# Quantised cross-attention of a six-stage decoder on one core: maxima on VectorE, scores read from PSUM by ScalarE

## The chip, the cores and the metric

One NeuronCore of a Trainium2 chip runs the whole program. The metric is the device time of one execution in microseconds (us); the median of several executions is given.

## What is computed

Two decoder layers, each with self-attention, cross-attention and a feed-forward part, every part followed by a residual add and a layer norm: six stages on x of 2 x 256 tokens and 256 columns. The change is in stage 5, the quantised cross-attention:

```python
q = _fq_sym(q * scale, axis=-1)       # round(q / s) * s, s = max|q| / 127 per token and head
k = _fq_sym(k, axis=-1)
v = _fq_sym(v, axis=2)
attn = softmax(einsum('bhqd,bhkd->bhqk', q, k))
attn = _fq_unsigned(attn, axis=-1)    # round(attn / s) * s, s = max / 255 per row
out = einsum('bhqk,bhkd->bhqd', attn, v) @ Wp + bp
```

All 512 queries look at all 1024 context tokens, with 16 heads of 16 columns. Since a row's largest probability becomes 255, exp(score - max + ln 255) written as a whole number is the quantised probability; the sum of the exponentials isn't needed for the scale of a step, only to divide the result.

## The kernel before, in words

The program is written engine by engine, with semaphores by hand; each engine works through its list in order. Stages 1 to 4 end at about 233 us, stage 5 runs from there to about 346 us, stage 6 (64 experts) fills the rest.

Stage 5 is cut into 64 **units**: a block i of 128 queries (4 of them) and one head h (16). A unit's way:

- TensorE, `scores(u)` (line 1098): two matmuls of 128x512 into two banks of PSUM, units in turn in banks 0-1 and 2-3. The scores are products of whole numbers (the queries' rounded values); the query scale `qsc` is still to be multiplied. They wait for the maximum of unit u-2, which has emptied the two banks. TensorE issues them three units ahead of its loop.
- VectorE, `maximum(u)` (line 1629): one custom instruction that multiplies by `qsc`, stores the scores in SBUF (`sx`, three buffers in turn) and gives the row's maximum; an instruction that reads its accumulator follows. It waits for the scores, and for the exponential of unit u-3, which frees `sx`.
- GpSimd (line 563): the bias, ln 255 minus the maximum.
- ScalarE (line 724): the exponential of `sx` with that bias, written as int16 into `px` (PX = 4 buffers in turn), with the row's sum, read from the accumulator by a second instruction. It waits for the bias, and for the turn of unit u-4 out of the same `px` buffer.
- The turn (128 queries x 1024 keys become 8 blocks of keys x queries), in one of two ways. By DMA: SyncE issues one DMA transpose (line 407) from `px` to `pTx` (PT = 6 buffers in turn) and waits for `px` and for the products that free `pTx`. Or "by scalar", for every ninth unit from unit 4 and the last two: TensorE transposes into banks 4 and 5 (line 1108) and ScalarE copies to `pTx` (`evac_px`, line 747).
- TensorE, `apply(m)` (line 1123): for two units at once, 16 matmuls with the quantised values, into bank 6 or 7.

Per block come the division by the sums (`turn_z`, `spread_z`, `normalise`), the projection, the residual add and the norm (`add`, `norm_stats`, `norm_scale`), between units of the next block. The blocks' quantised queries are themselves turned by DMA (`turn_queries`, line 393): blocks 0 and 1 in stage 4, blocks 2 and 3 in stage 5, before the transposes of unit 8 and unit 11 in SyncE's list. Block 3's queries need stage 4's last norm, so TensorE projects them in its step 10 (`queries`, line 798), behind the scores of unit 13; VectorE adds a bias (line 1523) and quantises them behind the maximum of unit 12.

Of the kernel before, what the change touches and what calls it, by code (L numbers as in the profile page):

```python
# [58 lines left out]
PT = 6  # L59
SHARE = ((4,), 9)  # L60
GROUP = 4
# [7 lines left out]
def build(nc, t, out):  # L69

    with ExitStack() as ctx:
# [160 lines left out]

        sx = carve("a", 2 * N, [3, B * M])
        pTx = [carve(where, at + k * KT * P // 2, [KT * P], I16)
# [38 lines left out]
        def by_scalar(u):  # L273

            return u % SHARE[1] in SHARE[0] or u >= TT * HX - 2

        def query_bank(i):

            return bank(6)[:, D:2 * D] if i == 1 else bank(7)[:, 0:D]

        def unit5(u):
# [146 lines left out]
        def _(pool):  # L428
# [116 lines left out]
            for n in range(1, STAGES + 1):  # L545
# [13 lines left out]
                if n == 5:  # L559

                    for u in range(TT * HX):
                        pool.wait_ge(sem("maxx_ready"), u + 1)
                        pool.tensor_scalar(nbx[:, u:u + 1], mxx[:, u:u + 1], -1.0, math.log(255.0),  # L563
                                           ALU.mult, ALU.add).then_inc(sem("biasx_ready"), 1)
# [29 lines left out]
        def _(act):  # L594
# [120 lines left out]
            def stage5():  # L715

                act.wait_ge(sem("o1_ps"), len(items1) // 2)
                for u in range(TT * HX):
                    i, h = unit5(u)
                    act.wait_ge(sem("biasx_ready"), u + 1)  # L720
                    if u >= PX:

                        px_free(act, u - PX)
                    act.activation(px[:, u % PX, :], sx[:, u % 3, :], ACT.Exp, bias=nbx[:, u:u + 1],  # L724
                                   accum_out=zx[:, i, h:h + 1]).then_inc(sem("px_ready"), 1)
# [68 lines left out]
        def _(pe):  # L794
# [291 lines left out]
            def stage5():  # L1086
# [3 lines left out]
                def scores(u):  # L1090
                    i, h = unit5(u)
                    if u >= 2:

                        pe.wait_ge(sem("maxx_ready"), u - 1)
                    if h == HEADS[0]:
                        pe.wait_ge(sem("queries_turned"), 32 * (i + 1))
                    for half in range(2):
                        mm = pe.matmul(bank(2 * (u % 2) + half), qTx[i][:, h * P:(h + 1) * P].bitcast(BF16),  # L1098
                                       kTx[:, h // 2, half * 512:(half + 1) * 512], start=True, stop=True)
                    mm.then_inc(sem("sx_ps"), 1)  # L1100
# [50 lines left out]
                for u in range(units + 3):  # L1151
# [32 lines left out]
                    if u == units + 2:  # L1184
# [4 lines left out]
                        mm.then_inc(sem("zfx_ps"), 1)  # L1189
                        pe.wait_ge(sem("maxx_ready"), units)  # L1190
                        for i in range(TT - 1):
# [3 lines left out]
                    if u == units - 2:  # L1195

                        pe.wait_ge(sem("maxx_ready"), units - 1)
                        for i in range(TT - 1):
                            pe.wait_ge(sem("x_ready"), nth(5, i))
                            for c in range(DC):  # L1200
                                mm = pe.transpose(bank(i // 2)[:, D * (i % 2) + c * P:D * (i % 2) + (c + 1) * P],
                                                  x_tok[1][:, i, c * P:(c + 1) * P], ident[:])
# [79 lines left out]
        def _(dve):  # L1282
# [338 lines left out]
            def stage5():  # L1621
                def maximum(u):

                    dve.wait_ge(sem("sx_ps"), u + 1)
                    i, h = unit5(u)
                    if u >= 3:

                        dve.wait_ge(sem("px_ready"), u - 2)
                    dve.tensor_tensor_reduce(sx[:, u % 3, :], bank(2 * (u % 2), 2), zero[:].broadcast_to([P, B * M]),  # L1629
                                             qsc[:, i, h:h + 1], LOWEST, ALU.add, ALU.max,  # L1630
                                             mxx[:, u:u + 1]).then_inc(sem("maxx_ready"), 1)

# [47 lines left out]
                for i in range(TT - 1):  # L1680
                    dve.wait_ge(sem("xT_ps"), nth(5, max(i, 1)))
                    slot = bank(i // 2)[:, D * (i % 2):D * (i % 2) + D].rearrange("p (c t) -> p c t", c=DC)
                    dve.tensor_copy(xT[1][:, :, i * P:(i + 1) * P], slot).then_inc(sem("xT_ready"), 1)
# [112 lines left out]
```

## Time and profile before

| | us |
|---|---|
| median of 3 runs | 448.67 (448.04 to 448.78) |
| the profiled execution, its own time | 446.82 |
| its span, first to last instruction | 445.0 |

| engine | busy us | share of the span |
|---|---|---|
| TensorE, matmuls | 369.6 | 83% |
| TensorE, weight loads | 219.1 | 49% |
| VectorE | 304.7 | 68% |
| ScalarE | 211.5 | 48% |
| GpSimd | 110.5 | 25% |

The shares are means over six stages with different limits: in stage 6 TensorE is full (9 tenths in each of the last slices) while VectorE is at 2 to 3 tenths; in stage 5 TensorE stands at 7 to 8 tenths, VectorE and ScalarE at 8 to 9 and the DMA engines at 7 to 9. The chain of waits that ended last goes through TensorE for 55% of the span, VectorE 14%, DMA 10%, ScalarE 6%. In the rows below, PE is TensorE, DVE VectorE, ACT ScalarE, POOL GpSimd, SPq the queue of SyncE; a group's row reads: line, engine, operation, out<-in with shapes, xcount | busy us, mean ns of one | idle us of the engine just before them, and what ended it.

### The profile page before, as it was taken

Reading aid. Unit: us, or ns where it says so; the run is one execution under the profiler, and the core shown is the slowest. Engines: PE = TensorE matmul, PEld = TensorE weight load, DVE = VectorE, ACT = ScalarE, POOL = GpSimd, SP = SyncE. Lnnn points to the kernel's source line nnn. Section 1 sums busy time; section 2 is a strip of 40 time slices with the busy share of each in tenths; the row PEclk is TensorE's granted clock in tenths of the full one; section 3 lists DMA queues with packets and bytes.
Section 4 is the critical chain, followed back from the end, with each engine's and each line's share of the span. In section 5 each row is a group of like instructions: output and inputs, shape, how many; then the busy total and the mean of one; then the engine's idle time right before and its main releaser. Section 6 shows DMA issues by size and latency. Waiting matters only on the chain.

```text
span 445.0 us, 6798 instructions
## 1 busy us (share of the span) xinstructions
PE 369.6 (83%) x2355; PEld 219.1 (49%) x2379; DVE 304.7 (68%) x636; ACT 211.5 (48%) x540; POOL 110.5 (25%) x214
## 2 busy tenths in 40 slices
PE   5978859599987999989976657778669897999993
PEld 2535547444443566657753323335337444556662
DVE  3896988989624587889779888998993652222335
ACT  2781412462245665765526758988985420111100
POOL 8237778648471000000111101211120000000002
PEclk9998996889999599999989886896998999999997
DMA  8994111850000000020026789997998004122111
GB/s 255 292 371 91 1 3 2 330 236 1 0 1 0 1 2 1 1 49 0 4 47 104 143 156 157 159 159 144 161 174 233 3 5 149 40 55 47 49 47 47
DMA packets 81857, 41.42 MB, mean 93 GB/s; under 512 B 70496, under 2 KB 77600, under 8 KB 81376
## 3 DMA queue, kind: packets, MB, share of 16 engines
q1 hardware_dynamic: 79520, 40.93, 38.2%
q0 software_dynamic: 2304, 0.07, 1.5%
q8 instruction: 19, 0.31, 0.3%
q14 instruction: 14, 0.11, 0.1%
HBM read 21.58 MB, written 2.88 MB: 55 GB/s over the span
## 4 chain that ended last, share of the span: by engine, by line
PE 55%; DVE 14%; DMA 10%; issue 9%; POOL 6%; ACT 6%; SPq 0%; POOLq 0%; DVEq 0%; ACTq 0%
PE ps L798 28%; PE ps L1254 6%; DMA area_b<-area_a 6%; PE ps L1037 5%; PE ps L1048 4%; POOL deltas L508 4%; DVE area_a L1629 3%; ACT area_a L724 3%; PE ps L970 2%; PE ps L1031 2%; PE ps L1098 2%; ACT area_a L699 2%; DMA area_b<-deltas 2%; DMA deltas<-entry_w,small 1%; DVE stats L1374 1%
## 5 line engine op out<-in xcount | busy, mean ns | idle before, releaser
L1629 DVE CUSTOM_DVE_ANT_0 area_a<-ps,zero,small 128x1024 f32<-128x1024 f32 x64 | 79.5, 1274 | 7.8 <-PE ps L1098 3.8
L724 ACT ACTIVATE area_a<-area_a,small 128x1024 int16<-128x1024 f32 x64 | 73.1, 1143 | 22.6 <-POOL small L563 13.7
L699 ACT ACTIVATE area_a<-ps,small 128x256 f32<-128x256 f32 (+1 forms) x128 | 52.0, 430 | 31.8 <-DVE small L1571 28.0
L798 PE MATMUL ps<-xT_odd,early 128*128 128x512 f32 (+2 forms) x136 | 58.3, 571 | 0.9 <-DVE area_b L1711 0.8
L486 POOL TENSOR_SCALAR var_eps<-meanvar 128x1 f32<-128x1 f32 x24 | 7.0, 293 | 198.5 <-DVE meanvar L1375 198.3
L1711 DVE TENSOR_TENSOR area_b<-ps,area_b 128x512 f32<-128x512 f32 x16 | 11.0, 690 | 50.5 <-ACT area_b L773 50.5
L1571 DVE TENSOR_REDUCE small<-ps 128x4 f32<-128x1024 f32 (+1 forms) x24 | 29.3, 1222 | 20.2 <-PE ps L1037 17.3
L773 ACT ACTIVATE area_b<-ps 128x512 f32<-128x512 f32 x16 | 9.5, 596 | 61.9 <-PE ps L798 61.9
L798 PEld LDWEIGHTS ps<-xT_odd,early 128*128 128x128 f32 x136 | 24.9, 190 | 26.3 <-issue 22.3
L798 PE MATMUL ps<-area_b,xT_even 128*128 128x512 f32 x64 | 31.4, 637 | 5.2 <-ACT area_b L676 5.2
L563 POOL TENSOR_SCALAR small<-small 128x1 f32<-128x1 f32 x64 | 12.7, 198 | 84.5 <-DVE small L1629 84.4
L1580 DVE COPY area_b<-ps 128x512 f32<-128x512 f32 x48 | 30.9, 680 | 1.7 <-PE ps L1048 1.5
L1254 PE MATMUL ps<-area_a,area_b 128*128 128x256 f32 x128 | 29.8, 380 | 2.6 <-DVE area_b L1740 2.6
L1098 PE MATMUL ps<-area_b,area_a 128*128 128x512 bf16 x58 | 18.6, 398 | 15.4 <-DVE small L1629 14.6
L1123 PE MATMUL ps<-area_b 128*32 128x128 f16 x512 | 23.0, 240 | 8.3 <-DMA area_b<-area_a 7.4
L1254 PEld LDWEIGHTS ps<-area_a,area_b 128*128 128x128 f32 x128 | 24.2, 190 | 11.3 <-issue 7.8
L508 POOL DMA_INDIRECT deltas<-entry_w,small x16 | 26.2, 1636 | 13.9 <-DVE small L1334 8.0
L1048 PE MATMUL ps<-ident,area_a 128*128 128x128 f32 x192 | 29.1, 298 | 0.5 <-DVE area_b L1580 0.4
L1037 PE MATMUL ps<-area_a,area_b 32*128 32x256 f32 (+1 forms) x160 | 29.2, 475 | 0.0
L1048 PEld LDWEIGHTS ps<-ident,area_a 128*128 128x128 f32 x192 | 22.7, 151 | 12.8 <-issue 6.6
L1123 PEld LDWEIGHTS ps<-area_b 128*32 128x32 f16 x512 | 17.0, 106 | 22.3 <-issue 20.4
L699 ACT ACTIVATION_READ_ACCUMULATOR area_a<-ps,small 128x1 f32 x128 | 27.4, 214 | 0.0
(278 smaller groups left out, 637.9 us busy)
## 6 DMA issues: line engine op xcount, KB each, us to landing
early<-in_w_up_dram SPq DMA_DIRECT2D x1, 4096.0 KB, 13.5
area_b<-gates_out SPq DMA_DIRECT2D x16, 256.0 KB, 3.1
deltas<-area_b SPq DMA_DIRECT2D x1, 2112.0 KB, 17.7
area_b<-deltas SPq DMA_DIRECT2D x2, 1024.0 KB, 5.8
area_a<-in_w_down_dram SPq DMA_DIRECT2D x1, 2048.0 KB, 11.5
early<-in_ctxT_dram SPq DMA_DIRECT2D x1, 1024.0 KB, 13.1
early<-in_ctx_dram SPq DMA_DIRECT2D x1, 1024.0 KB
area_b<-area_a SPq DMA_TRANSPOSE x59, 3.3
```

The source lines that it names most:

```text
L508: pool.indirect_dma_start(out=deltas, out_offset=bass.IndirectOffsetOnAxis(ap=place[:, j:j + 1], axis=0), in_=entry_w[:, j, :], in_offset= ...
L699: a = act.activation(p1[:, n % 2, x * nk * P:(x + 1) * nk * P], scores1(n)[:, x * nk * P:(x + 1) * nk * P], ACT.Exp, bias=nmx1[:, n % 2, x ...
L724: act.activation(px[:, u % PX, :], sx[:, u % 3, :], ACT.Exp, bias=nbx[:, u:u + 1], accum_out=zx[:, i, h:h + 1]).then_inc(sem("px_ready"), 1)
L798: mm = pe.matmul(dst, lhsT(c), rhs(c), start=start and c == 0, stop=stop and c == DC - 1, **kw)
L1037: mm = pe.matmul(dst, qT1[rows, c, i * P:(i + 1) * P], kT1[rows, c, heads, kt * P:(kt + 1) * P], start=False, stop=b == nk - 1)
L1048: mm = pe.transpose(bank(4 + x)[:, y * P:(y + 1) * P], p1[:, n % 2, (4 * x + y) * P:(4 * x + y + 1) * P], ident[:])
L1098: mm = pe.matmul(bank(2 * (u % 2) + half), qTx[i][:, h * P:(h + 1) * P].bitcast(BF16), kTx[:, h // 2, half * 512:(half + 1) * 512], start= ...
L1123: mm = pe.matmul(dst, ivh[:, k * HX + h, :], p[:, k * P:(k + 1) * P], start=first and k == 0, stop=not first and k == KT - 1)
L1254: mm = pe.matmul(proj(i), hidden[:, g % 2, i * P:(i + 1) * P], w_down[:, g, :], start=g == 0 and i % 2 == 0, stop=g == NG - 1, skip_group_ ...
L1571: dve.tensor_reduce(nmx1[:, n % 2, 0:8 // nk], scores1(n).rearrange("p (h k) -> p h k", k=nk * P), AX.X, ALU.max, negate=True).then_inc(se ...
L1580: dve.tensor_copy(pT1[:, n % 4, 4 * x * P:4 * (x + 1) * P], bank(4 + x)).then_inc(sem("pT1_ready"), 1)
L1629: dve.tensor_tensor_reduce(sx[:, u % 3, :], bank(2 * (u % 2), 2), zero[:].broadcast_to([P, B * M]), qsc[:, i, h:h + 1], LOWEST, ALU.add, A ...
```

## The change

1. VectorE takes only the maximum, straight from PSUM, with its sign turned (`tensor_reduce`); `sx` is gone.
2. ScalarE reads the scores from PSUM, with `qsc` as the scale of the exponential beside the bias. GpSimd's bias multiplies the (negated) maximum by `qsc`.
3. The scores of a unit lie in three places in turn, banks 0-1, 2-3 and 4-5. `scores(u)` waits for the exponential of unit u-3 instead of the maximum of unit u-2.
4. Only units 62 and 63 are turned by TensorE and ScalarE. Units 4, 13, 22, 31, 40, 49 and 58 are now turned by DMA as well.
5. At the end of the stage the first three blocks' transposes go to banks 2 and 3, and wait for an exponential instead of a maximum.

```diff
-SHARE = ((4,), 9)
...
-            return u % SHARE[1] in SHARE[0] or u >= TT * HX - 2
+            return u >= TT * HX - 2
...
+        def scores5(u):
+
+            return bank(2 * (u % 3), 2)
...
-                        pool.tensor_scalar(nbx[:, u:u + 1], mxx[:, u:u + 1], -1.0, math.log(255.0),
+                        i, h = unit5(u)
+                        pool.tensor_scalar(nbx[:, u:u + 1], mxx[:, u:u + 1], qsc[:, i, h:h + 1], math.log(255.0),
...
-                    act.activation(px[:, u % PX, :], sx[:, u % 3, :], ACT.Exp, bias=nbx[:, u:u + 1],
+                    act.activation(px[:, u % PX, :], scores5(u), ACT.Exp, bias=nbx[:, u:u + 1], scale=qsc[:, i, h:h + 1],
...
-                    if u >= 2:
-
-                        pe.wait_ge(sem("maxx_ready"), u - 1)
+                    if u >= 3:
+
+                        pe.wait_ge(sem("px_ready"), u - 2)
...
-                        mm = pe.matmul(bank(2 * (u % 2) + half), qTx[i][:, h * P:(h + 1) * P].bitcast(BF16),
+                        mm = pe.matmul(scores5(u)[:, half * 512:(half + 1) * 512], qTx[i][:, h * P:(h + 1) * P].bitcast(BF16),
...
-                        pe.wait_ge(sem("maxx_ready"), units)
+                        pe.wait_ge(sem("xT_ready"), nth(5, TT - 2))
...
-                        pe.wait_ge(sem("maxx_ready"), units - 1)
+                        pe.wait_ge(sem("px_ready"), units - 2)
...
-                    i, h = unit5(u)
-                    if u >= 3:
-
-                        dve.wait_ge(sem("px_ready"), u - 2)
-                    dve.tensor_tensor_reduce(sx[:, u % 3, :], bank(2 * (u % 2), 2), zero[:].broadcast_to([P, B * M]),
-                                             qsc[:, i, h:h + 1], LOWEST, ALU.add, ALU.max,
-                                             mxx[:, u:u + 1]).then_inc(sem("maxx_ready"), 1)
+                    dve.tensor_reduce(mxx[:, u:u + 1], scores5(u), AX.X, ALU.max, negate=True).then_inc(sem("maxx_ready"), 1)
```

What moves in the engines' lists shows on TensorE around the first block change (line 1098, in the new kernel 1101, are the scores; 1123, now 1126, the products with the values; 1108 the turn of a probability unit; 1131 and 1137, now 1134 and 1140, the turn and spread of the sums). Before:

```order
L1123 MATMUL ps<-area_b 32x128 [waits turned_3,turned_2,qx_ready]
L1123 MATMUL ps<-area_b 32x128 x15
L1098 MATMUL ps<-area_b 128x512 [waits maxx_ready]
L1098 MATMUL ps<-area_b 128x512
L1131 MATMUL ps<-ident,small 16x128 [waits sumsx_out,rzx_ready]
L1098 MATMUL ps<-area_b 128x512 [waits maxx_ready]
L1098 MATMUL ps<-area_b 128x512
L1123 MATMUL ps<-area_b 32x128 [waits turned_1,turned_0]
L1123 MATMUL ps<-area_b 32x128 x15
L1098 MATMUL ps<-area_b 128x512 [waits maxx_ready]
L1098 MATMUL ps<-area_b 128x512
L1108 MATMUL ps<-ident_b,area_a 128x128 [waits pTx_act,px_ready]
```

And now:

```order
L1126 MATMUL ps<-area_b 32x128 [waits turned_1,turned_0,qx_ready]
L1126 MATMUL ps<-area_b 32x128 x15
L1101 MATMUL ps<-area_b 128x512 [waits px_ready]
L1101 MATMUL ps<-area_b 128x512
L1134 MATMUL ps<-ident,small 16x128 [waits sumsx_out,rzx_ready]
L1101 MATMUL ps<-area_b 128x512 [waits px_ready]
L1101 MATMUL ps<-area_b 128x512
L1126 MATMUL ps<-area_b 32x128 [waits turned_3,turned_2]
L1126 MATMUL ps<-area_b 32x128 x15
L1101 MATMUL ps<-area_b 128x512 [waits px_ready]
L1101 MATMUL ps<-area_b 128x512
L1140 MATMUL ps<-rzTx,pair_rows 128x128 [waits rzTx_ready]
```

The order is the same but for the turn, which is gone; each unit's scores wait for ScalarE (`px_ready`) instead of VectorE (`maxx_ready`).

SyncE's list from unit 0 on (line 407, now 409, a unit's probabilities; 393, now 395, the queries of blocks 2 and 3). Before:

```order
L407 DMA_TRANSPOSE area_b<-area_a 128x8x128 [waits px_ready] x5
L407 DMA_TRANSPOSE area_b<-area_a 128x8x128 [waits ox_ps,px_ready] x2
L393 DMA_TRANSPOSE area_b<-area_a 128x8x128 [waits qstack_ready]
L393 DMA_TRANSPOSE area_b<-area_a 128x8x128
L407 DMA_TRANSPOSE area_b<-area_a 128x8x128 [waits ox_ps,px_ready] x3
L393 DMA_TRANSPOSE area_a<-area_a 128x8x128 [waits qstack_ready]
L393 DMA_TRANSPOSE area_a<-area_a 128x8x128
L407 DMA_TRANSPOSE area_b<-area_a 128x8x128 [waits ox_ps,px_ready] x45
```

And now:

```order
L409 DMA_TRANSPOSE area_b<-area_a 128x8x128 [waits px_ready] x6
L409 DMA_TRANSPOSE area_b<-area_a 128x8x128 [waits ox_ps,px_ready] x2
L395 DMA_TRANSPOSE area_b<-area_a 128x8x128 [waits qstack_ready]
L395 DMA_TRANSPOSE area_b<-area_a 128x8x128
L409 DMA_TRANSPOSE area_b<-area_a 128x8x128 [waits ox_ps,px_ready] x3
L395 DMA_TRANSPOSE area_a<-area_a 128x8x128 [waits qstack_ready]
L395 DMA_TRANSPOSE area_a<-area_a 128x8x128
L409 DMA_TRANSPOSE area_b<-area_a 128x8x128 [waits ox_ps,px_ready] x51
```

One transpose more stands ahead of the queries of block 2, and 51 instead of 45 behind those of block 3.

## Rows read from the trace of the kernel before

**Rows 1.** The page, part 5: groups of the quantised stage and their idle time.
```profile
L1629 DVE CUSTOM_DVE_ANT_0 area_a<-ps,zero,small 128x1024 f32<-128x1024 f32 x64 | 79.5, 1274 | 7.8 <-PE ps L1098 3.8
L724 ACT ACTIVATE area_a<-area_a,small 128x1024 int16<-128x1024 f32 x64 | 73.1, 1143 | 22.6 <-POOL small L563 13.7
```

**Rows 2.** Windows of the quantised stage: busy by engine, clock, DMA share, GB/s.
```profile
core 0: us, PE busy (x) PEld busy (x) DVE busy (x) ACT busy (x) POOL busy (x), PEclk, DMA share, GB/s
233.00:261.00 28.00, 17.05 (x156) 8.43 (x159) 25.84 (x56) 18.01 (x30) 4.46 (x18) 0.91 0.70 123
261.00:336.00 75.00, 55.91 (x576) 28.62 (x583) 65.61 (x116) 65.76 (x116) 12.09 (x56) 0.86 0.92 159
```

**Rows 3.** Line 407, the DMA transposes of probabilities: issue duration, who waited, landing.
```profile
L407 SPq DMA_TRANSPOSE area_b<-area_a x55: 1231/1283/2644, 235.8 to 334.9; - x55
...
  ACT area_a L724: 8.5, 11
...
DMA to landing us min/median/max: 3.0/3.3/4.8
```

**Rows 4.** Timeline of SyncE's queue: start, us from first start to last end, count.
```profile
258.37 2.62 SPq L393 DMA_TRANSPOSE area_a<-area_a  x2
...
261.09 75.01 SPq L407 DMA_TRANSPOSE area_b<-area_a  x45
```

**Rows 5.** The same queue in five stretches between transposes that TensorE made.
```profile
267.83 9.56 SPq L407 DMA_TRANSPOSE area_b<-area_a  x6
...
281.69 8.69 SPq L407 DMA_TRANSPOSE area_b<-area_a  x6
...
294.43 8.89 SPq L407 DMA_TRANSPOSE area_b<-area_a  x6
...
308.89 8.12 SPq L407 DMA_TRANSPOSE area_b<-area_a  x6
...
317.73 12.28 SPq L407 DMA_TRANSPOSE area_b<-area_a  x8
```

**Rows 6.** DMA queues: all of 308.9 to 317 us; instruction loads of 261 to 336 us.
```profile
q1 hardware_dynamic: 5289, 1.32, 86.1%
...
q8 instruction: 5, 0.08, 0.5%
```

**Rows 7.** Groups by form: VectorE maxima; ScalarE from SBUF or PSUM, with scalars.
```profile
L1571 DVE TENSOR_REDUCE small<-ps 128x4 f32<-128x1024 f32 x16 | 19.6, 1222 | 11.6 <-PE ps L1037 11.5
...
L688 ACT ACTIVATE area_a<-ps,head_sel 128x512 f32<-128x512 f32 x8 | 4.8, 688 | 4.9 <-PE ps L798 4.9
...
L653 ACT ACTIVATE area_a<-area_a,small 128x512 f32<-128x512 f32 x4 | 2.9, 717 | 2.3 <-issue 2.3
...
L636 ACT ACTIVATE area_a<-ps,bvx 128x512 f32<-128x512 f32 x4 | 2.7, 673 | 1.0 <-PE ps L798 1.0
...
L661 ACT ACTIVATE area_a<-ps 128x512 f32<-128x512 f32 x4 | 2.4, 597 | 3.5 <-PE ps L907 3.1 <-issue 0.4
```

**Rows 8.** Timeline at the last block's queries and the unit after them.
```profile
252.45 0.93 PE L1098 MATMUL ps<-area_b,area_a 128*128 128x512 bf16 x2 [0.60 <-DVE small L1629]
...
255.19 0.42 DVE L1523 TENSOR_TENSOR area_b<-ps,bqx 128x256 f32<-128x256 f32 x1 [1.60 <-PE ps L798]
...
258.26 1.28 DVE L1629 CUSTOM_DVE_ANT_0 area_a<-ps,zero,small 128x1024 f32<-128x1024 f32 x1
...
259.61 1.03 PE L1098 MATMUL ps<-area_b,area_a 128*128 128x512 bf16 x2 [3.01 <-DVE small L1629]
...
259.86 1.15 ACT L724 ACTIVATE area_a<-area_a,small 128x1024 int16<-128x1024 f32 x1 [2.55 <-POOL small L563]
```

**Rows 9.** Timeline near the end of the stage.
```profile
321.10 0.60 PE L1098 MATMUL ps<-area_b,area_a 128*128 128x512 bf16 x2
...
331.93 1.00 ACT L747 ACTIVATE area_b<-ps 128x1024 int16<-128x1024 int16 x1
...
335.88 1.14 ACT L724 ACTIVATE area_a<-area_a,small 128x1024 int16<-128x1024 f32 x1
```

More of the change, by code:

```diff
@@ L231, in build @@
         zx, rzx = tiny([TT, HX]), tiny([TT, HX])
-        sx = carve("a", 2 * N, [3, B * M])
         pTx = [carve(where, at + k * KT * P // 2, [KT * P], I16)
@@ L1200, in stage5 @@
                             for c in range(DC):
-                                mm = pe.transpose(bank(i // 2)[:, D * (i % 2) + c * P:D * (i % 2) + (c + 1) * P],
+                                mm = pe.transpose(bank(2 + i // 2)[:, D * (i % 2) + c * P:D * (i % 2) + (c + 1) * P],
                                                   x_tok[1][:, i, c * P:(c + 1) * P], ident[:])
@@ L1681, in stage5 @@
                     dve.wait_ge(sem("xT_ps"), nth(5, max(i, 1)))
-                    slot = bank(i // 2)[:, D * (i % 2):D * (i % 2) + D].rearrange("p (c t) -> p c t", c=DC)
+                    slot = bank(2 + i // 2)[:, D * (i % 2):D * (i % 2) + D].rearrange("p (c t) -> p c t", c=DC)
                     dve.tensor_copy(xT[1][:, :, i * P:(i + 1) * P], slot).then_inc(sem("xT_ready"), 1)
```

## The prediction

> **What bounds the kernel now.** I read the page's groups first, then the windows of the quantised stage (five, from 233 us to about 336 us), then the queue of SyncE, then the timeline at two places. The groups [rows 1] seem to say VectorE: 64 maxima of 1274 ns, and only 7.8 us idle before them, against 22.6 us before ScalarE's 64 exponentials. But the windows [rows 2] show no full engine: from 261 to 336 us VectorE and ScalarE are each busy 65.6 and 65.8 us of 75, TensorE 55.9, while the 16 DMA engines stand at 0.92. The work that fills them is the DMA transposes: 55 of the 64 units of probabilities, one issue taking 1283 ns of SyncE in the median, and landing 3.3 us after its start; ScalarE waited 8.5 us for landings [rows 3], since the exponential of unit u overwrites the buffer that unit u-4 was turned out of.
>
> So the question is how often that queue was empty. After the last block's queries (258.37) SyncE issues 45 transposes in 75.01 us, 1.67 us each [rows 4]; the other six units of that stretch are turned by TensorE. In five stretches where the queue was hardly ever empty, 32 issues take 47.54 us, **1.486 us each** [rows 5]. The best of them, 8.12 us for six (1.353 us each), is the one in which the DMA list holds the kernel's own queue alone; in the whole 75 us there are five loads of instructions of 16 KB [rows 6], and the other stretches, which have one each, are the slow ones. The excess of those four over 1.353 us an issue is 47.54 - 32 x 1.353 = 4.2 us, about 1.06 us for each load.
>
> **The change, part by part.**
>
> *Six more DMA transposes behind the last queries (units 13, 22, 31, 40, 49 and 58), one more before (unit 4).* SyncE's 45 issues become 51. At 1.486 us each they take 75.8 us where 45 took 75.0: **+0.8 us**. That is the core of the forecast: in the trace of before, the queue's idle time beside a unit turned by TensorE was about as large as the issue that now fills it. Bounds: from below 51 x 1.353 + 5 x 1.06 = 74.3 us (-0.7), every issue at the best pace and as many instruction loads as before; from above the pace over the whole stretch, 1.67, for all 51, 85.0 us (+10.0), which nothing but a new stall would give, since its idle time is tied to the units skipped; a mid-way value of 1.58, the slowest of the five stretches (9.56 us for six is 1.593), gives 81.2 us (+6.2). I take 1.486 because it is the mean of stretches that are already what the whole stage becomes. Unit 4's issue falls into the part before 261 us, where SyncE stands waiting for the queries of blocks 2 and 3: nothing.
>
> The Trainium skill gives another price for the same transfer (DMA: Bandwidth & Descriptors, section "Latency and other measured facts"): a DMA transpose moves 261 GB/s where its middle dimension is not contiguous. By it a unit's 256 KB would take an estimated 1.0 us and 51 of them 51 us, so that this queue would not bound the stage at all; the 1.353 us of the best stretch, 194 GB/s, speaks against it here.
>
> *Seven turns less for TensorE and seven copies less for ScalarE.* Such a copy takes 1.00 us [rows 9]. They lie beside the queue: 7 us off ScalarE, which had 9 us of the 75 to spare. Nothing on the path, save at the end (below).
>
> *ScalarE reads PSUM and takes a second scalar per partition.* PSUM in place of SBUF, with a bias in both: 673 against 717 ns, -44. A scale from a tensor over none: 688 against 597 ns, +91 [rows 7]. So 1143 + 91 - 44 = 1190 ns, +47 ns for 64 units, +3.0 us, less than the copies give back. It is hidden while 1.19 us stays under the queue's 1.486; without that cover it costs its 3.0 us.
>
> *VectorE reduces instead of scaling, adding and storing.* A reduction of 1024 columns from PSUM takes 1222 ns in stage four [rows 7] against 1274: -3.3 us over 64, and the instruction that read the accumulator goes. VectorE still needs the scores, so it waits instead: nothing. GpSimd's scalar operation takes its factor from a tensor; no row shows that price, between 0 and the 91 ns of ScalarE's scale; I take 0, it has slack in each unit.
>
> *The new wait.* TensorE's scores of unit u+3 waited for the maximum of unit u+1; now they wait for the exponential of unit u, since they overwrite its place in PSUM. Behind them in TensorE's order stand the products with the values, which free the buffers that the queue fills, and VectorE waits for the scores. One turn of that circle, for three units: exponential 1.19 and its accumulator (estimate 0.1), scores 0.60 at 2.4 GHz or 1.03 at 1.2 GHz [rows 9, 8], maximum to the start of the exponential 1.60 - 1.28 + 1.22 = 1.54 (258.26 to 259.86 [rows 8], with the reduction in place of the old maximum). That is 3.4 us at the high clock and 3.9 at the low one, 1.15 and 1.29 us a unit, so the queue's 1.486 still bounds; but each block's lumps (projection, residual and statistics, about 1 us each) have only 0.6 to 1.0 us per turn to vanish in. I take **+0.4 us** for them; ends 0 and +3.1 (the VectorE lump, 1.03 us from three pieces of 0.42, 0.43 and 0.18, paid in full at the three block changes; an estimate).
>
> *Startup.* The queries of the last block come behind the scores of unit 13 (252.45), VectorE adds their bias at 255.19 and is done at 258.26, when SyncE goes on [rows 8, 4]. These scores waited for the maximum of unit 11, 1.28 + 1.22 = 2.5 us after the start of the maximum of unit 10; now for the exponential of unit 10, 1.54 + 1.19 + 0.1 = 2.8 us after it: **+0.3 us** (0 to +1).
>
> *End.* The last exponential began at 335.88, behind the copy of unit 58 at 331.93 [rows 9] and a late landing. Now it needs the landing of unit 59, two issues before the last one (334.9 [rows 3]): 334.9 - 2 x 1.353 + 3.3 = 335.5, **-0.4 us**. What follows is unchanged.
>
> Sum: 0.8 + 0.4 + 0.3 - 0.4 = **+1.1 us**. The profiled execution took 446.82 us (span 445.0), so this one should take 447.9; it lies 1.85 us under the median of the runs, 448.67, to which I add the same: **449.8 us**. About 0.2%, 0.9 us, is what a measurement of this kernel can tell from no change; the forecast lies just beyond it.
>
> **The rivals.**
>
> *A, coupling.* The wait on the exponential replaces two waits that let TensorE run ahead by five units; now it runs ahead by three. If the lumps are paid in full and the low clock lasts longer (granted clock 0.86 in the 75 us [rows 2]), +3.1 in place of +0.4: 452.5 us. For it: VectorE idled 7.8 us before its maxima even at the old depth [rows 1]. Against: the circle is 3.4 to 3.9 us where three issues take 4.5. Chance 0.22.
>
> *B, faster: the queue never runs dry.* Place: SyncE's 51 issues; price: 74.3 us for them, -0.7, nothing for coupling and the startup: -0.7 - 0.4 = -1.1, 447.6 us; one instruction load fewer, as TensorE and ScalarE have fewer instructions, makes -2.2, 446.5 us. It decides from 1.46 us an issue downwards. For it: much of the excess is tied to a count of loads, not of transposes. Against: no stretch with a load went under 1.44. Chance 0.25.
>
> *C, the transposes were slowed by SBUF traffic.* VectorE no longer writes 4 KB of a partition per unit, nor does ScalarE read it back. If the transposes then ran clear of it, the circle at the low clock would bound: 51 x 1.29 = 65.8 us, -9.2, with startup and end 439.4 us. The skill's 261 GB/s of above would let this happen. Against: the issue itself takes at least 1231 ns of SyncE [rows 3] even alone. Chance 0.03.
>
> *D, a new stall* in the startup or an exponential dearer than 1190 ns, by up to the +6.2 above: 453 to 456 us. Chance 0.10.
>
> **How the numbers follow.** The forecast case, 0.40, spreads over 448.6 to 451.2 and lies about half inside 0.2%. Faster by over 0.2% (under 447.8): most of B and C, 0.24. Within: 0.28. Slower: the other half of the forecast case, A and D, 0.48. Range 446.5 to 453.0: B's lower end to A; C and most of D are left out.
>
> **What would show it.** Right: SyncE's last stretch holds 51 transposes in 75 to 77 us; the exponential takes 1.18 to 1.20 us, the reduction about 1.22; ScalarE's idle time goes over to the DMA as releaser; TensorE's scores wait for ScalarE. A shows as VectorE waiting for scores and the queue with gaps; B as issues of 1.40 us; C as issue durations under 1.2 us. The forecast is wrong if the 51 issues take over 79 us or under 74, or if the time moved outside 233 to 340 us.

## The result, and the profile after

| | kernel before | changed kernel |
|---|---|---|
| median of 20 runs each | 447.29 us (442.67 to 453.36) | 452.09 us (446.15 to 456.4) |
| profiled execution, its own time (span) | 446.82 (445.0) | 449.34 (447.6) |

The changed kernel is slower: ratio 1.0086, 95% interval 1.0053 to 1.0118, some 3.8 us where +1.1 was forecast. Ratios are formed without the runs that lie over 1.5% above the fastest of their kernel, so a ratio can lie beside that of the two medians (here 1.0107); both are given below, and the profiled executions of kernels 2 and 7 are such left-out runs.

First the page's groups of the stage, as in [rows 1] (line, engine, operation, count | busy us, mean ns | idle us before them and who ended it):

```profile
L727 ACT ACTIVATE area_a<-ps,small 128x1024 int16<-128x1024 f32 x64 | 76.7, 1202 | 30.2 <-POOL small L566 16.9
L1628 DVE TENSOR_REDUCE small<-ps 128x1 f32<-128x1024 f32 x64 | 76.5, 1219 | 13.2 <-PE ps L1101 12.2
...
L566 POOL TENSOR_SCALAR small<-small 128x1 f32<-128x1 f32 x64 | 17.5, 273 | 82.8 <-DVE small L1628 82.6
```

The durations came as forecast: exponential 1202 ns (forecast 1190), reduction 1219 (1222). GpSimd's bias, costed at nothing, takes 273 ns where the constant factor took 198. The idle time before the exponentials rose from 22.6 to 30.2 us, before the maxima from 7.8 to 13.2. It did not go over to the DMA as the forecast had it: GpSimd's part rose from 13.7 to 16.9, that of late landings from 8.5 to 12.5.

The windows, as in [rows 2], and line 409, as in [rows 3]:

```profile
233.00:261.00 28.00, 15.47 (x135) 7.14 (x127) 25.13 (x40) 18.34 (x30) 5.61 (x18) 0.89 0.78 138
261.00:336.00 75.00, 51.86 (x517) 23.85 (x525) 61.50 (x65) 61.10 (x105) 15.27 (x54) 0.88 1.04 176
```

```profile
L409 SPq DMA_TRANSPOSE area_b<-area_a x62: 1231/1287/2283, 235.1 to 335.3; - x62
...
  ACT area_a L727: 12.5, 11
  PE ps L1126: 4.1, 5
...
DMA to landing us min/median/max: 3.1/3.3/4.9
```

The DMA share of the 75 us went from 0.92 to 1.04 with the six transposes more; TensorE, VectorE and ScalarE are each less busy than before, and the time is longer. No compute engine is full, and 1.04 is not the most that the DMA engines reach (kernel 1 below has 1.08 over as long a stretch): the loss is waiting.

Then SyncE's queue, as in [rows 4]:

```profile
257.63 2.61 SPq L395 DMA_TRANSPOSE area_a<-area_a  x2
...
260.34 76.29 SPq L409 DMA_TRANSPOSE area_b<-area_a  x51
```

Fifty-one transposes in 76.29 us, inside the 75 to 77 that the prediction named. And what TensorE's scores waited for (us, times; weight loads and matmuls together): in the changed kernel

```profile
  ACT area_a L727: 78.8, 92
```

and in the kernel before

```profile
  DVE small L1629: 52.2, 61
```

The waits for the maximum have become waits for the exponential, and the sum grew by half. (A weight load and its product can wait through the same time, so the sums serve for comparison only.)

I cut both spans at the same four events: the first exponential (234.57 before, 233.75 after), the first transpose behind the last queries (261.09, 260.34), the last transpose's issue (334.9, 335.3) and the last exponential (335.88 [rows 9], 337.35).

| stretch, us | before | after | difference | forecast |
|---|---|---|---|---|
| up to the first exponential | 234.6 | 233.7 | -0.8 | 0 |
| "startup", to the first transpose behind the last queries | 26.5 | 26.6 | +0.1 | +0.3 |
| "queue", to the last issue | 73.8 | 75.0 | +1.2 | +0.8 and +0.4 |
| "end", to the last exponential | 1.0 | 2.0 | +1.0 | -0.4 |
| the rest | 109.1 | 110.2 | +1.1 | 0 |

The sum is +2.6, the difference of the spans. "Stage" below is startup, queue and end: 101.3 before, 103.6 after.

The timeline of a block change shows the form of a stop (start, us, engine, line, operation [idle before <- releaser]):

```profile
306.00 0.85 PE L1101 MATMUL ps<-area_b 128*128 128x512 bf16 x2 [0.58 <-ACT area_a L727]
306.63 1.91 PE L801 MATMUL ps<-wpx,attTx 128*128 128x256 f32 x4
...
308.48 1.04 PE L1126 MATMUL ps<-area_b 128*32 128x128 f16 x16
...
308.50 1.21 ACT L727 ACTIVATE area_a<-ps,small 128x1024 int16<-128x1024 f32 x1
308.59 0.42 DVE L1642 TENSOR_TENSOR res<-ps,x_even 128x256 f32<-128x256 f32 x1 [0.48 <-PE ps L801]
...
309.45 1.11 PE L1101 MATMUL ps<-area_b 128*128 128x512 bf16 x3
...
310.17 3.49 DVE L1628 TENSOR_REDUCE small<-ps 128x1 f32<-128x1024 f32 x3 [0.48 <-PE ps L1101]
...
311.79 1.20 ACT L727 ACTIVATE area_a<-ps,small 128x1024 int16<-128x1024 f32 x1 [2.00 <-POOL small L566]
```

Scores at 306.00, and their next ones only at 309.45: between them the projection (1.91 us, at the low clock) and the products. The scores that follow could not be made before the projection, as they wait for a later exponential, and now it stands in front of them. VectorE waits for them (310.17), ScalarE for VectorE: exponentials at 308.50 and 311.79, 3.29 us apart where the queue takes one in 1.5. It is an example and not the account of the whole loss: the same two exponentials, of units 45 and 46, are 2.25 us apart in kernel 1 below and 1.33 in kernel 5, whose stage is as long as this one.

### The profile page after: what moved, and what is told of

Same layout as the page of the kernel before. It is cut to its first block, busy times and chain, and to the rows that moved or that the text cites. A ratio compares the mean times of both kernels' runs of the same rounds, so it can differ in the third digit from the quotient of the medians.

```text
span 447.6 us, 6555 instructions
## 1 busy us (share of the span) xinstructions
PE 365.5 (82%) x2300; PEld 214.0 (48%) x2323; DVE 301.9 (67%) x572; ACT 208.4 (47%) x533; POOL 115.1 (26%) x214
## 4 chain that ended last, share of the span: by engine, by line
PE 49%; DMA 15%; DVE 13%; ACT 8%; POOL 6%; issue 6%; SPq 2%; POOLq 0%; ACTq 0%; DVEq 0%
PE ps L801 26%; DMA area_b<-area_a 9%; PE ps L1257 6%; ACT area_a L727 6%; PE ps L1040 5%; PE ps L1051 4%; POOL deltas L510 4%; DMA bvx<-in_bvx_dram 3%; DVE small L1628 3%; PE ps L973 2%; PE ps L1034 2%; SPq L344 2%; DMA area_b<-deltas 2%; ACT area_a L702 2%; DMA deltas<-entry_w,small 1%
## 5 line engine op out<-in xcount | busy, mean ns | idle before, releaser
L727 ACT ACTIVATE area_a<-ps,small 128x1024 int16<-128x1024 f32 x64 | 76.7, 1202 | 30.2 <-POOL small L566 16.9
L1628 DVE TENSOR_REDUCE small<-ps 128x1 f32<-128x1024 f32 x64 | 76.5, 1219 | 13.2 <-PE ps L1101 12.2
L702 ACT ACTIVATE area_a<-ps,small 128x256 f32<-128x256 f32 (+1 forms) x128 | 52.0, 431 | 28.8 <-DVE small L1574 27.8
L1574 DVE TENSOR_REDUCE small<-ps 128x4 f32<-128x1024 f32 (+1 forms) x24 | 29.3, 1221 | 17.1 <-PE ps L1040 16.9
L566 POOL TENSOR_SCALAR small<-small 128x1 f32<-128x1 f32 x64 | 17.5, 273 | 82.8 <-DVE small L1628 82.6
L1101 PE MATMUL ps<-area_b 128*128 128x512 bf16 x58 | 20.7, 435 | 13.9 <-ACT area_a L727 13.3
L1051 PE MATMUL ps<-ident,area_a 128*128 128x128 f32 x192 | 28.2, 292 | 0.5 <-DVE area_b L1583 0.4
L1040 PE MATMUL ps<-area_a,area_b 32*128 32x256 f32 (+1 forms) x160 | 27.4, 451 | 0.0
L1126 PE MATMUL ps<-area_b 128*32 128x128 f16 x512 | 21.5, 233 | 4.1 <-DMA area_b<-area_a 4.1
```

The costliest lines, as they stand in the source:

```text
L702: a = act.activation(p1[:, n % 2, x * nk * P:(x + 1) * nk * P], scores1(n)[:, x * nk * P:(x + 1) * nk * P], ACT.Exp, bias=nmx1[:, n % 2, x ...
L727: act.activation(px[:, u % PX, :], scores5(u), ACT.Exp, bias=nbx[:, u:u + 1], scale=qsc[:, i, h:h + 1], accum_out=zx[:, i, h:h + 1]).then_ ...
L1040: mm = pe.matmul(dst, qT1[rows, c, i * P:(i + 1) * P], kT1[rows, c, heads, kt * P:(kt + 1) * P], start=False, stop=b == nk - 1)
L1051: mm = pe.transpose(bank(4 + x)[:, y * P:(y + 1) * P], p1[:, n % 2, (4 * x + y) * P:(4 * x + y + 1) * P], ident[:])
L1101: mm = pe.matmul(scores5(u)[:, half * 512:(half + 1) * 512], qTx[i][:, h * P:(h + 1) * P].bitcast(BF16), kTx[:, h // 2, half * 512:(half + ...
L1126: mm = pe.matmul(dst, ivh[:, k * HX + h, :], p[:, k * P:(k + 1) * P], start=first and k == 0, stop=not first and k == KT - 1)
```

## The experiments

Each kernel was run in five rounds beside the kernel before. Runs with neighbouring numbers on one chip: 1 to 4, 5 to 8, 9 and 10, 11 and 12. The last four columns are of the profiled execution, with the cuts of above.

| kernel | median us (runs) | over the median of before | ratio, 95% interval | mean clock of the runs | startup | queue | end | stage |
|---|---|---|---|---|---|---|---|---|
| before (one median for each chip) | 446.5, 446.9, 445.1, 445.9 | | 1 | 0.936 | 26.5 | 73.8 | 1.0 | 101.3 |
| changed | 452.1 (20) | 1.011 | 1.0086, 1.0053 to 1.0118 | 0.917 | 26.6 | 75.0 | 2.0 | 103.6 |
| 1 all by DMA | 449.2 (12) | 1.006 | 0.9989, 0.9947 to 1.0032 | 0.933 | 26.5 | 73.3 | 1.0 | 100.8 |
| 2 six left out | 448.4 (12) | 1.004 | 1.0003, 0.9958 to 1.0048 | 0.920 | 27.9 | 72.2 | 1.4 | 101.5 |
| 3 ten product buffers | 451.8 (12) | 1.012 | 1.0123, 1.0079 to 1.0166 | 0.918 | 28.0 | 74.5 | 1.9 | 104.4 |
| 4 projection first | 453.7 (6) | 1.016 | 1.0166, 1.0113 to 1.0219 | 0.915 | 27.9 | 73.4 | 2.0 | 103.3 |
| 5 1 with the wait | 451.4 (6) | 1.010 | 1.0116, 1.0057 to 1.0174 | 0.914 | 28.2 | 73.2 | 2.2 | 103.5 |
| 6 no scale | 452.7 (12) | 1.013 | 1.0101, 1.0055 to 1.0146 | 0.919 | 27.0 | 72.5 | 0.9 | 100.4 |
| 7 six buffers | 449.4 (12) | 1.006 | 1.0051, 1.0008 to 1.0093 | 0.922 | 27.9 | 73.4 | 0.2 | 101.5 |
| 8 1 with six buffers | 451.2 (6) | 1.010 | 1.0112, 1.006 to 1.0163 | 0.927 | 26.5 | 72.2 | 1.5 | 100.2 |
| 9 5 with fillings | 449.7 (12) | 1.010 | 1.0092, 1.0055 to 1.0129 | 0.940 | 27.8 | 74.6 | 0.9 | 103.3 |
| 10 1 with fillings | 447.3 (12) | 1.005 | 1.0054, 1.0018 to 1.0091 | 0.937 | 26.5 | 73.3 | 0.8 | 100.6 |
| 11 queries first | 449.0 (12) | 1.007 | 1.0072, 1.0033 to 1.0111 | 0.917 | 26.1 | 74.1 | 2.4 | 102.6 |
| 12 11 and six buffers | 448.3 (12) | 1.005 | 1.0025, 0.9977 to 1.0072 | 0.926 | 25.9 | 72.1 | 0.7 | 98.8 |

**1, the transposes alone; 5, the wait alone.** Kernel 1 is the kernel before with one line changed, kernel 5 adds the new wait to it beside the old ones:

```diff
 def by_scalar(u):
-    return u % SHARE[1] in SHARE[0] or u >= TT * HX - 2
+    return u >= TT * HX - 2
```

```diff
 # kernel 5 only, in scores(u)
         pe.wait_ge(sem("maxx_ready"), u - 1)
+    if u >= 3:
+        pe.wait_ge(sem("px_ready"), u - 2)
```

> The kernel before with one part of the change alone: every unit but the last two is turned by DMA; VectorE still scales and stores, ScalarE reads SBUF, TensorE still waits for the maximum of two units back. Queue theory (the cost of the change is the six extra transposes): the stretch of 51 issues takes 75 to 77 us, and the kernel is slower than before by 1 to 4 us, as much as the whole change. Coupling theory (the cost is the new wait of the scores for ScalarE): 51 issues in under 75.5 us and the kernel within 1 us of before, or faster.

> The kernel of e1 (all units but the last two by DMA, all else as before) with one wait more: the scores of unit u+3 also wait for the exponential of unit u, as in the change. e1's stage, from the first to the last exponential, took 100.8 us, the change's 103.6. Wait theory (the new wait makes the cost): the stage takes 102.5 to 104 us and the kernel is slower than before by 0.4 to 1.2%. Duration theory (the wait is covered; the cost is the dearer exponential, 1204 for 1143 ns, and bias, 273 for 198 ns): the stage stays at 100.5 to 101.5 us.

The queue of kernel 1 and its window, then the queue of kernel 5 (its last issue alone took 1.8 us):

```profile
260.45 74.54 SPq L407 DMA_TRANSPOSE area_b<-area_a  x51
```

```profile
260.00:335.00 75.00, 48.19 (x528) 23.56 (x536) 65.63 (x118) 61.24 (x110) 12.27 (x56) 0.96 1.08 181
```

```profile
266.73 75.00 SPq L407 DMA_TRANSPOSE area_b<-area_a  x51
```

Fifty-one issues in 74.54 us, **less than the 75.01 that 45 took** [rows 4]: the units that TensorE turned had left gaps in the queue at least as long as an issue. The ratio holds no change; the median, 1.006, leaves room for half a per cent. Kernel 5 differs from it by the one wait, the reading of PSUM by VectorE and the maximum as before: its ratio is 1.0116, its stage 103.5 against 100.8, +2.7 us. That is the changed kernel's stage (103.6), made without a touch on VectorE's or ScalarE's instructions.

Where these 2.7 us lie is another matter. Three pairs differ in the wait (the changed kernel differs from kernel 1 in its instructions as well; kernel 10 is kernel 1 with the filling product of below):

| wait's price, us | startup | queue | end | stage |
|---|---|---|---|---|
| changed over 1 | +0.1 | +1.7 | +1.0 | +2.8 |
| 5 over 1 | +1.7 | -0.1 | +1.2 | +2.7 |
| 9 over 10 | +1.3 | +1.2 | +0.1 | +2.7 |

The sum is steady, its place is not, and in kernel 5 the queue lost nothing. Each row rests on one execution of each kernel. For the sum there is more: with the wait, four buffers and 51 issues, five kernels (changed, 3, 4, 5, 9) have stages of 103.3 to 104.4 us, and the four kernels without the wait 100.2 to 101.3. The exceptions are kernel 11, with its queries ahead (102.6), and kernel 6, with the cheaper exponential (100.4).

**2, six transposes left out; 3, more product buffers; 4, the projection ahead of the scores** (all on the changed kernel). Kernel 2 omits the transposes of units 13, 22, 31, 40, 49 and 58 (`if not by_scalar(u) and not left_out(u)` in SyncE's list, with the waits counted accordingly), so that their products read what lies in the buffer. The others:

```diff
-PT = 6
+PT = 10
```

```diff
+if u > HX and u % HX == 10:
+    project(u // HX - 1)
 if u + 3 < units:
     scores(u + 3)
```

> The changed kernel with the transposes of units 13, 22, 31, 40, 49 and 58 left out (their products use old data; exponentials, scores and products stay), so 45 issues stand behind the last queries. Queue theory: the stage gets shorter by nearly what six issues cost, 6 x 1.5 = 9 us less what ScalarE and the circle through the scores allow, at least 3 us. Coupling theory: since the waits of the scores stay as they are, the gain is under 2 us.

> The changed kernel with ten buffers for the turned probabilities instead of six, so that SyncE never waits for TensorE's products. If the gaps seen in the queue at units 44, 46 and 60 come from products that are late (behind scores that wait for ScalarE), this returns 0.5 to 2 us. If the queue itself is the bound, it returns less than 0.5 us.

> The changed kernel with each block's projection ahead of the scores of its step on TensorE instead of behind them: it then runs while TensorE waits for ScalarE. Coupling theory: the stop of some 3 us before the exponential of unit 46 and that before unit 29 shrink, 1 to 3 us back. Queue theory: under 0.5 us, since the queue has work waiting at these places.

Without the six transposes the changed kernel is at 1.0003, as kernel 1 is without the wait (0.9989): by the ratios it is the two together that cost. This is suggested and not shown. By the medians the two simply add (1.006 and 1.004 against 1.011), and in kernel 2 nobody turns the six units, so it also lacks the work that TensorE and ScalarE did for them in the kernel before. Its stage, 101.5, is 2.1 us shorter than the changed kernel's, between what the two theories named (at least 3, under 2), although six issues of 1.5 us are gone: the queue is not the only bound. Product buffers are not it (1.0123, the queue 74.5; 0.5 to 2 us back were expected if they were). Moving the projection ahead gave nothing back, where the coupling theory expected 1 to 3 us; the ratio is rather higher (1.0166, its interval just meets the changed kernel's). Its exponentials of units 45 and 46 are 2.12 us apart and the queue took 73.4, so the stop of above is softened, but neither the stage (103.3) nor the runs gain by it; why is open.

**6, exponential and bias without the scale; 7, six buffers of probabilities in place of four; 8, the same on kernel 1.** In 6 the scores are not scaled (`scale=qsc[...]` gone, the bias's factor 1.0). In 7 and 8:

```diff
-PX = 4
+PX = 6
```

(with `px` at another place, in 8 as a list of pieces).

> The changed kernel without the query scale: ScalarE's exponential has no tensor scale and GpSimd's bias takes a constant, so the scores are not scaled. Waits and order as in the change. Duration theory: exponential near 1110 ns, bias near 200 ns, the circle shorter by some 0.17 us, and the stage back at 100.5 to 101.5 us. Wait theory: the circle of 3.5 us shrinks by 5%, so less than a third of the 2.8 us returns; the stage takes 102.5 to 103.5 us.

> The changed kernel with six buffers for the exponentials instead of four, at the place of the scores that are no longer stored: ScalarE may run further ahead of the landings, and since the scores now wait for ScalarE, TensorE and VectorE too. If late landings (12.5 us of ScalarE's idle) are what the new wait passes on, the stage shrinks to 101 to 102.5 us. If the stops come from TensorE's own order (projection ahead of scores), it stays at 103 to 104.

> The kernel of e1 with six buffers for the exponentials. With the queue as its only bound, the stage falls from 100.8 us to 98.5 to 100 us, since late landings no longer reach ScalarE; a candidate that beats both kernels. If ScalarE and TensorE in the part before 261 us bound as well, it stays within 0.5 us of e1.

Kernel 6's exponential takes 1111 ns in place of 1202, and its stage is the shortest with the wait and four buffers, 100.4, but the kernel's ratio stays at 1.0101: what the profiled execution gains in the stage is not in the runs. I can't settle this. The dearer exponential and bias therefore stay a possible part of the loss beside the wait, though not a needed one: kernel 5 has the old durations and loses the 2.7 us. Kernel 6's execution ran 114.7 us after the last exponential's start where before took 109.1, with the low clock from 339.9 to 346.7 and from 374.0 to 377.4 us, where the kernel before had the high one. This tail, which the change touches only in its first few microseconds, takes anything from 108.6 to 115.5 us in the fourteen profiled executions (the longest is kernel 7's), more than the effect sought; so a stage is compared here with a stage, and totals by the runs. Kernel 7 gives back some: 1.0051. The wait for landings, 12.5 us before the exponentials, is gone (0.4), but GpSimd as releaser went from 16.9 to 27.6: 10.7 of the 12.1 us moved on to the maximum and its scores. Kernel 8 gained nothing: stage 100.2, but ratio 1.0112; where the rest of it went is not known (111.6 us after the stage).

**9 and 10, the waits filled.** The mean clock of the runs goes with the time. Among the 20 runs of the changed kernel the fastest (446.15 us) had 0.929, the two with the lowest clocks, 0.904 and 0.907, took 455.96 and 454.72; and kernels with the wait on the exponential had 0.914 to 0.926, those without 0.927 to 0.936. So a second theory stood beside the circle: TensorE waits more, is granted less clock, and that is what costs. To tell them apart kernel 9 (on 5) and kernel 10 (on 1) put a product that nobody reads ahead of the waits:

```diff
+if u >= 8:
+    j, g = unit5(u - 1)
+    pe.matmul(bank(4), qTx[j][:, g * P:(g + 1) * P].bitcast(BF16), kTx[:, g // 2, 0:512], start=True, stop=True)
 if u >= 2:
     pe.wait_ge(sem("maxx_ready"), u - 1)
```

> The kernel before with every unit but the last two turned by DMA and with the added wait of the scores on the exponential of three units before (the run with the added wait alone took 451.4 us, clocks of its runs 0.910 to 0.918), and now one more product of TensorE a unit, ahead of these waits: 512 columns into a bank that nothing reads (some 0.22 us at 2.4 GHz, 0.43 us at 1.2 GHz), 56 of them. It only fills time in which TensorE would stand waiting. Theory 'the granted clock': the wait costs time because TensorE stands idle in it and is then granted the low clock more often; with the gaps filled the mean clock goes back to 0.925 or more and the time to 447 to 449.5 us. Theory 'the circle': the wait costs time because the exponential, the scores and the maximum follow each other; the filling changes nothing in that or adds to it, 451 to 454 us, and the clock stays at 0.91 to 0.92.

> The same filling product on the kernel before with every unit but the last two turned by DMA, without the added wait (that one took 449.2 us, mean clock 0.933). Theory 'the granted clock': the clock goes up to 0.94 and the time falls to 445 to 448 us, less than both kernels. Theory 'the circle': nothing to gain, 449 us, or up to 3 us more where the filling product delays scores that VectorE waits for.

Kernel 9's window and queue:

```profile
264.00:339.00 75.00, 58.95 (x556) 25.88 (x556) 65.30 (x116) 60.18 (x106) 11.98 (x55) 0.98 1.10 178
```

```profile
263.70 75.85 SPq L407 DMA_TRANSPOSE area_b<-area_a  x51
```

and kernel 10's queue:

```profile
260.34 74.59 SPq L407 DMA_TRANSPOSE area_b<-area_a  x51
```

The filling did what it should to the clock, 0.98 in that stretch and 0.940 over the runs, and **the wait still costs 2.7 us of the stage**: 103.3 against kernel 10's 100.6, the same as 5 against 1. The clocks of the two stages are alike, 0.95 and 0.95, where kernels 5 and 1 had 0.85 and 0.95. So the wait is a cause by itself, without the low clock. Of the total the picture is less sharp. The 449.7 us lie at the upper edge of what the clock theory named (447 to 449.5), but the kernel before is faster on this chip too, and over it kernel 9 is at 1.010 as kernel 5 was. 9 against 10 is 449.7 against 447.3, +2.5 us, while the filling alone seems to cost something too (10 at 1.0054, 1 at 0.9989, intervals that overlap a little; the medians, 1.005 and 1.006, show no such cost). Whether part of the remaining microsecond or two is the clock's stays open.

**11 and 12, the queries ahead of the scores.** The table shows the startup at 27.8 to 28.2 in six kernels with the wait (27.0 in the seventh, with the cheaper exponential) and 26.5 in all without; the changed kernel's profiled execution is the exception. Its timeline there:

```profile
251.52 1.20 ACT L727 ACTIVATE area_a<-ps,small 128x1024 int16<-128x1024 f32 x1 [2.17 <-POOL small L566]
...
252.87 0.61 PE L1101 MATMUL ps<-area_b,area_a 128*128 128x512 bf16 x2 [3.06 <-ACT area_a L727]
...
253.31 1.03 PE L801 MATMUL ps<-wqx,xT_even 128*128 128x256 f32 x4
...
254.45 0.42 DVE L1526 TENSOR_TENSOR area_b<-ps,bqx 128x256 f32<-128x256 f32 x1 [1.06 <-PE ps L801]
```

and kernel 7's, which has the same order:

```profile
251.76 1.20 ACT L727 ACTIVATE area_a<-ps,small 128x1024 int16<-128x1024 f32 x1 [2.17 <-POOL small L566]
...
253.11 1.03 PE L1101 MATMUL ps<-area_b,area_a 128*128 128x512 bf16 x2 [3.05 <-ACT area_a L727]
...
253.94 1.91 PE L801 MATMUL ps<-wqx,xT_even 128*128 128x256 f32 x4
...
255.96 0.42 DVE L1526 TENSOR_TENSOR area_b<-ps,bqx 128x256 f32<-128x256 f32 x1 [2.33 <-PE ps L801]
```

The scores wait 3.06 us for the exponential, and the projection of the last queries stands behind them. At the high clock (1.03 us) that is just made good; at the low one (1.91 us, as it has in the kernel before and in 1 as well) VectorE gets the queries 1.3 us later (4.20 us after the exponential's start in place of 2.93), and SyncE issues nothing until then. So the projection was put ahead:

```diff
+if u == AT_3:
+    queries(TT - 1)
 if u + 3 < units:
     scores(u + 3)
```

> The changed kernel, with the projection of the last block's queries (four products of 256 columns, 1.03 us at 2.4 GHz, 1.91 us at 1.2 GHz) put ahead of the scores in its step on TensorE, so that it no longer stands behind their wait for the exponential. In the changed kernel's trace these scores waited 3.06 us for the exponential, the queries began at 253.31 although their input was turned by 249.4, and VectorE, idle, took them up at 254.45. SyncE issues nothing of the stage until they are turned: from the first exponential to the first transpose behind them it took 26.5 to 26.6 us in the kernels without the added wait and in the profiled run of the changed one, but 27.1 to 28.2 in the seven other profiled kernels with it. Theory 'the startup pays for the wait': that stretch becomes 25.0 to 26.0 us, and the kernel gains 1 to 2.5 us: 449.5 to 451 against the changed kernel's 452.1, ratio to the kernel before 1.003 to 1.006. Rival 'the queue bounds and takes it back': the stretch is shorter and the 51 issues behind it longer by as much; ratio 1.008 to 1.012. Rival 'the block changes pay': nothing moves in the startup, ratio as before.

> The same with six in place of four buffers of probabilities (alone they gave 449.4 us, ratio 1.0051, against the changed kernel's 1.0086). If the startup and the exponential's wait for a landing are two separate prices of the change, the gains add: 447 to 448.5 us, ratio 1.000 to 1.003, the change brought back to the kernel before. If both only give back the same wait, no better than with the buffers alone: ratio 1.004 to 1.006. If the circle of exponential, scores and maximum is all there is, as in the kernel with the filled waits: 1.006 to 1.010.

```profile
249.67 1.03 PE L801 MATMUL ps<-wqx,xT_even 128*128 128x256 f32 x4
...
252.89 0.61 PE L1101 MATMUL ps<-area_b,area_a 128*128 128x512 bf16 x2 [2.19 <-ACT area_a L727]
...
253.33 0.41 DVE L1526 TENSOR_TENSOR area_b<-ps,bqx 128x256 f32<-128x256 f32 x1
...
256.84 2.71 SPq L395 DMA_TRANSPOSE area_a<-area_a  x2
```

The projection runs at 249.67, before the wait; the startup is 26.1 and 25.9, at the upper edge of the 25.0 to 26.0 expected and under that of every other kernel. Kernel 11's median over before is 1.007 where the changed kernel's is 1.011, but its ratio, 1.0072 (expected 1.003 to 1.006), can't be told from 1.0086. Kernel 12 has the shortest stage of all, 98.8:

```profile
260.63 73.42 SPq L409 DMA_TRANSPOSE area_b<-area_a  x51
```

```profile
L727 ACT ACTIVATE area_a<-ps,small 128x1024 int16<-128x1024 f32 x64 | 76.5, 1199 | 25.4 <-POOL small L566 24.5 <-DMA area_b<-area_a 0.6
```

and a ratio of 1.0025 (0.9977 to 1.0072): nearest to before of all kernels with the whole change, as expected if the gains add (1.000 to 1.003), but not faster than before. No version beat both kernels.

## Why the prediction came out as it did

The sign was right and 452.09 us lies in the range; the size was not. The forecast was +1.1 us, the runs show +3.8 (by the medians +4.8). That the time still lies in the range is in part luck: the forecast was added to 448.67 us, the median of three runs, and twenty gave 447.29. The range reached 4.3 us above its base; 4.3 above 447.29 is 451.6, and 452.09 would lie just outside. Rival A, coupling, came nearest (+3.8 us in all), though not in the place that it named, as the second point says.

- **Six more transposes, +0.8 us: too dear.** Kernel 1 shows -0.5 (74.54 against 75.01). The 1.486 us an issue came from five stretches, four of them with an instruction load; kernel 1 made 50 intervals in 73.3 us, 1.466 each. For this term rival B had the better price (-0.7).
- **The new wait: here the forecast failed.** It stands in three terms, +0.4 for the lumps, +0.3 for the startup and -0.4 for the end, +0.3 us in sum. Measured are 2.7, 2.7 and 2.8 us of stage (kernels 5 over 1, 9 over 10, changed over 1). I compared the mean circle of three units (3.4 to 3.9 us) with three issues of the queue (4.5), found it covered, and let what is left vanish in the difference. The stage does not run by means: every place where work arrives in a lump or late (the last block's queries, a projection, the last units) now waits for an exponential, with less made in advance. That this is why is my reading, from the timelines shown; kernel 11 bears it out for the startup (26.1 us), and kernel 4, which moved the projections, gave nothing back. For the queue alone, which +0.4 (at most +3.1) was about, the three pairs show -0.1, +1.2 and +1.7. Rival A put its whole price there, at the three block changes; at the most 1.7 us lay in the queue, and in kernel 5 none. Its signs were seen in the changed kernel: VectorE waited for scores (12.2 us by the row of above, 3.8 before), and the queue had four gaps, intervals of 1.81 to 2.22 us whose issue took no more than 1.29.
- **Startup, +0.3 us (0 to +1): right in mechanism, too small in size.** It showed +0.1 in the changed kernel's profiled execution, +0.5 in kernel 6's and +1.3 to +1.7 in six others. I took it at the wait's length and not with the projection behind it at the low clock.
- **End, -0.4 us: wrong sign.** Measured +1.0 in the profiled execution, and the end varies from 0.2 to 2.4 us. The landing of unit 59 was in time; what was late was the exponential of unit 62, behind scores that followed the third block's projection:

```profile
331.30 1.91 PE L801 MATMUL ps<-wpx,attTx 128*128 128x256 f32 x4
...
333.87 1.04 PE L1101 MATMUL ps<-area_b,area_a 128*128 128x512 bf16 x3
...
336.13 1.20 ACT L727 ACTIVATE area_a<-ps,small 128x1024 int16<-128x1024 f32 x1 [1.67 <-POOL small L566]
...
337.35 1.20 ACT L727 ACTIVATE area_a<-ps,small 128x1024 int16<-128x1024 f32 x1
```

- **The dearer exponential, +47 ns forecast, +59 measured; the bias, 0 forecast, +75 measured.** Hidden by the queue, I said. They lie in the circle as well, so once the circle counts they need not be free; the stage of kernel 6 hints at up to 3 us, its runs show nothing.
- **Rival C** falls: no transpose in any kernel took under 1230 ns of SyncE, though in the kernels with the change nothing reads or writes `sx` any more. The Trainium skill (DMA: Bandwidth & Descriptors, "Latency and other measured facts") gives 261 GB/s for a DMA transpose whose middle dimension is not contiguous. No run here tells whether this transfer is such a one; kernel 12's queue, the fastest, moved its 256 KB in 1.443 us, 182 GB/s.
- **Outside the stage, 0.** The rest took +1.1 us, and the mean clock of the runs fell from 0.936 to 0.917. Stage 6 is unchanged; I did not foresee that a wait in stage 5 could show there, and it isn't proved that it does: the tail varies by 6.9 us between profiled executions. What the runs' +3.8 us have beyond the stage's +2.3 stays open.
- **Two slips in the working.** The chance of "slower" should be 0.52 (half of 0.40, and 0.22 and 0.10), not 0.48. The upper value of +6.2 us goes with 1.593 us an issue, not with the 1.58 named beside it. Neither touches the forecast.

## What to carry to other kernels

When a wait for an early step of a pipeline (the maximum) becomes one for a late step (the exponential), don't compare mean circle and mean bound: ask how far ahead the engine could run before, and what stands behind the wait in its order at the places where work comes in lumps, at the start and at the end too. A fuller queue and a shorter run-ahead, made in one change, are to be tried one by one: here a test of each showed that the wait costs 2.7 us of the stage and the transposes nothing of it. Work that needs nothing of the wait (here the query projection) belongs ahead of the waiting instruction.

## What the runs showed of the hardware

- One unread product of 512 columns a unit, added to kernel 5, lifted the mean granted clock of the runs from 0.914 to 0.940, and that of some 75 us of the stage from 0.88 to 0.98 (TensorE busy for 58.95 of 75 us, in kernel 5 for 53.03 of 76); yet the stage was only 0.2 us shorter. Added to kernel 1 the same product changed little (runs 0.933 and 0.937, stage 0.95 and 0.95).
- More busy time did not go with more clock: kernel 1 had 0.96 over 75 us with TensorE busy for 48.19, the kernel before 0.86 with 55.91.
- A unit's DMA transpose costs SyncE 1.23 us at least, 1.29 in the median, in every kernel, and 50 intervals in a row came to 1.44 to 1.50 us each in the twelve kernels that have so many. The pace did not tell the kernels in which VectorE writes the scores to SBUF (1.44 to 1.49) from those in which it does not (1.44 to 1.50).
- GpSimd's multiply-add of one column takes 198 ns with a constant factor and 273 with one from a tensor; ScalarE's exponential of 1024 columns from PSUM 1111 ns without a scale per partition and 1202 with it.
